# State-space layers: the LayerNorm's scale and shift on ScalarE between the next group's taps, with the shift made on GpSimd

## The reference

```python
def ssm_layer(x, Wi, cw, cb, Wo, g, b):          # x: (16, 128, 256), fp32
    proj = x @ Wi                                # 256 -> 512 + 64 + 64
    xs, Bm, Cm = proj[..., :512], proj[..., 512:576], proj[..., 576:]
    xc = silu(conv1d(xs, cw, 4 taps, causal) + cb)
    # h = -0.5 * h + u_t b_t ; y_t = h c_t, over the 128 steps
    return layer_norm(y @ Wo + x, g, b)
def layer_norm(x, g, b, eps=1e-05):
    mu = jnp.mean(x, axis=-1, keepdims=True)
    var = jnp.mean((x - mu) ** 2, axis=-1, keepdims=True)
    return (x - mu) * jax.lax.rsqrt(var + eps) * g + b
```

## Time and profile before

| | us |
|---|---|
| runs | 1495.00, 1495.44, 1496.55 (median 1495.44) |
| the profiled execution: its own time | 1493.37 |
| its span | 1491.6 |
| busy in the span: PE / DVE / ACT / POOL | 1207.3 / 841.1 / 631.7 / 603.6 |

### The profile page before, as it was taken

One profiled execution on the slowest core, in us unless ns is written; L12 is line 12 of the kernel. 1 busy time (PEld: TensorE's weight loads), 2 busy tenths in 40 slices (PEclk: granted clock), 3 DMA queues, 4 the chain that ended last, 5 costly groups with the idle time before them and its releaser, 6 DMA issues. The chain is left out here.

```text
span 1491.6 us, 21444 instructions
## 1 busy us (share of the span) xinstructions
PE 1207.3 (81%) x7243; PEld 944.3 (63%) x7243; DVE 841.1 (56%) x1844; ACT 631.7 (42%) x1863; POOL 603.6 (40%) x612
## 2 busy tenths in 40 slices
PE   4999999999799999997367777747999995366632
PEld 3888888888577777776356666544666663355521
DVE  6888888888434545444364754543222221448885
ACT  2555555555254454454136556612222221246420
POOL 2276767665521433333444534412111112644531
PEclk9999999999899999999688987867999998679865
DMA  4001010110000000000150002031111113210000
GB/s 143 1 15 54 15 53 15 52 27 3 0 1 1 1 1 1 1 2 1 34 227 2 1 2 85 1 142 32 47 46 44 49 43 83 90 43 15 15 14 29
DMA packets 30492, 53.38 MB, mean 36 GB/s; under 512 B 5088, under 2 KB 23264, under 8 KB 28864
## 3 DMA queue, kind: packets, MB, share of 16 engines
q1 hardware_dynamic: 26704, 39.72, 7.9%
q0 software_dynamic: 3408, 9.31, 2.2%
q10 hardware_dynamic: 288, 3.15, 0.6%
HBM read 42.86 MB, written 9.31 MB: 35 GB/s over the span
## 5 line engine op out<-in xcount | busy, mean ns | idle before, releaser
L414 DVE SCALAR_TENSOR_TENSOR ssm_conv<-bank,conv_w,ssm_conv 128x508 f32<-128x508 f32 (+2 forms) x240 | 159.2, 727 | 9.6 <-ACT ssm_conv L350 9.6
L1468 PE MATMUL bank<-expert_raw,e_rows_t 128*128 x312 | 148.9, 601 | 1.2 <-ACT e_rows_t L1540 1.2
L303 PE MATMUL bank<-w_out,ssm_u 128*128 128x256 f32 x640 | 143.5, 382 | 0.0
L710 ACT ACTIVATE a_prob<-bank,a_neg_max 128x128 f32<-128x128 f32 x256 | 90.5, 367 | 100.8 <-DVE a_neg_max L751 100.8
L303 PEld LDWEIGHTS bank<-w_out,ssm_u 128*128 128x128 f32 x640 | 119.9, 190 | 17.9
L1180 ACT ACTIVATE expert_raw<-bank,x_neg_max 128x128 f32<-128x128 f32 x256 | 90.9, 377 | 80.9 <-DVE x_neg_max L1114 80.9
L808 POOL TENSOR_TENSOR a_prob<-a_prob,a_inv 128x512 f32<-128x512 f32 x64 | 66.1, 1040 | 131.3 <-DVE a_inv L756 131.3
L1038 POOL TENSOR_TENSOR expert_raw<-expert_raw,x_inv 128x512 f32<-128x512 f32 x64 | 66.8, 1043 | 113.2 <-DVE x_inv L1120 113.2
L1415 POOL DMA_INDIRECT e_rows<-z_rows,e_index x39 | 37.1, 951 | 177.4 <-PE bank L1463 170.5
L1665 DVE COPY e_h_t<-bank 128x512 f32<-128x512 f32 x39 | 27.0, 692 | 128.0 <-PE bank L1477 128.0
L508 POOL TENSOR_TENSOR act_t_lo<-ssm_turned,act_t_hi 128x512 fp32r<-128x512 f32 x40 | 51.5, 1289 | 97.8 <-ACT ssm_turned L375 97.8
(11 more groups left out here) (360 smaller groups left out, 3209.7 us busy)
## 6 DMA issues: line engine op xcount, KB each, us to landing
expert_raw<-in_experts_laid SPq DMA_DIRECT2D x6, 1536.0 KB, 10.8
y_rows<-e_y SPq DMA_DIRECT2D x39, 128.0 KB, 1.7
attn_raw<-in_attn_w_laid SPq DMA_DIRECT2D x4, 1024.0 KB, 7.5
w_in_raw<-in_L_attn_in_proj_w SPq DMA_DIRECT2D x5, 640.0 KB, 8.4
expert_raw<-in_experts_laid ACTq DMA_DIRECT2D x2, 1536.0 KB, 8.7
w_out<-in_L_attn_out_proj_w SPq DMA_DIRECT2D x5, 512.0 KB, 3.4
x_res<-in_x SPq DMA_DIRECT2D x4, 512.0 KB, 5.6
expert_raw<-in_ctx_t_laid SPq DMA_DIRECT2D x4, 512.0 KB, 6.7
```

The lines of the kernel that those rows point to most:

```text
L303: mm = pe.matmul(UWY[h][:, s * D:(s + 1) * D], u[:, g % 2, c, t:t + P], w_out[:, c, :], start=(c == 0), stop=(c == KI - 1))
L414: op = dve.scalar_tensor_tensor(out=acc, in0=xs, scalar=conv_w[:, c, TAPS - 1 - back:TAPS - back], in1=acc, op0=ALU.mult, op1=ALU.add)
L710: e = act.activation(prob[:, m % 4, i, :], S[m % 2][:, i * P:(i + 1) * P], ACT.Exp, bias=neg_max[:, m % 4, i:i + 1], accum_out=total[:, m ...
L1468: mm = pe.matmul(bank[:, :], rows_t[:, t % 2, k, :], W[:, bass.ds(at + (column + k * FFN), FFN)], start=(k == 0), stop=(k == KD - 1))
```

## The change

DVE's four L450 instructions go. POOL makes minus the mean (a multiplication by a tile of -1), and after the `pow` the shift, minus the mean times rstd. ACT forms rstd * x + shift as four `ACT.Identity` instructions of 128x256 with scale and bias pointers, in the place `front` of the next group gives them: one behind tap 1, one behind tap 2, two behind tap 3. Where there is no next group they stand together: ahead of the last group's `copy_uw`, and at the very end. POOL, which waited for DVE's results by `z_ready`, now waits for ACT's by the same semaphore.

```diff
--- before.py
+++ after.py
@@ -179,6 +179,7 @@
     uw = sb("ssm_uw", [P, 2, 2 * D])
     res = sb("ssm_res", [P, 2, 2, D])
     stats, mv, ve = mem["stats"], mem["mv"], mem["ve"]
+    neg_mean, shift, neg_one = (sb("ssm_" + name, [P, GS]) for name in ("neg_mean", "shift", "neg_one"))
 
     bc_ready = sem("bc_ready")
     xs_ready = sem("xs_ready")
@@ -199,6 +200,7 @@
     aggr_ready = sem("aggr_ready")
     var_ready = sem("var_ready")
     rstd_ready = sem("rstd_ready")
+    neg_one_ready, neg_mean_ready, shift_ready = sem("neg_one_ready"), sem("neg_mean_ready"), sem("shift_ready")
     z_ready = sem("z_ready")
     zg_ready = sem("zg_ready")
     act_ready = sem("act_ready")
@@ -333,7 +335,13 @@
 
         @block.scalar
         def _(act):
-            def front(layer, g, first=False):
+            def normalise(layer, g, i):
+                n = layer * GROUPS + g
+                act.wait_ge(shift_ready, n * 2 + i // 2 + 1)
+                act.activation(res[:, i // 2, i % 2, :], res[:, i // 2, i % 2, :], ACT.Identity, bias=shift[:, i:i + 1],
+                               scale=ve[:, i:i + 1]).then_inc(z_ready, 1)
+
+            def front(layer, g, first=False, before=None):
 
                 n = layer * GROUPS + g
                 act.wait_ge(bc_ready, n + 1)
@@ -349,6 +357,9 @@
                         act.wait_ge(u_ready, n * KI - KI + c + 1)
                     nc.scalar.activation(conv[:, c, :], XS(c)[:, :], ACT.Identity, bias=conv_b[:, c:c + 1],
                                          scale=conv_w[:, c, TAPS - 1:TAPS]).then_inc(tap_last, 1)
+                    if before and c > 0:
+                        for i in ((0,), (1,), (2, 3))[c - 1]:
+                            normalise(*before, i)
 
             def silu(layer, g, chunks, first=False):
                 n = layer * GROUPS + g
@@ -381,13 +392,15 @@
                 first, last = layer_is(layer, 0), layer_is(layer, LAST)
                 for g in range(GROUPS):
                     ahead = (layer, g + 1, first) if g < GROUPS - 1 else None if last else (layer + 1, 0)
+                    before = (layer, g - 1) if g > 0 else None if first else (layer - 1, GROUPS - 1)
                     if ahead:
-                        front(*ahead)
-                    if ahead:
+                        front(*ahead, before=before)
                         silu(*ahead[:2], range(0, 2), *ahead[2:])
+                    else:
+                        for i in range(GS):
+                            normalise(*before, i)
                     copy_uw(layer, g, 0)
                     copy_uw(layer, g, 1)
-                    before = (layer, g - 1) if g > 0 else None if first else (layer - 1, GROUPS - 1)
                     if before:
                         copy_turned(*before, 0)
                     if ahead:
@@ -395,6 +408,8 @@
                     if before:
                         copy_turned(*before, 1)
             layers(act, layer_steps)
+            for i in range(GS):
+                normalise(LAST, GROUPS - 1, i)
             for h in range(2):
                 copy_turned(LAST, GROUPS - 1, h)
 
@@ -443,12 +458,6 @@
                     dve.wait_ge(aggr_ready, n * 4 + 2 * h + 2)
                     dve.tensor_scalar(ve[:, 2 * h:2 * h + 2], mv[:, 2 * h:2 * h + 2, 1], EPS, None,
                                       ALU.add).then_inc(var_ready, 1)
-                for h in range(2):
-                    dve.wait_ge(rstd_ready, n * 2 + h + 1)
-                    for s in range(2):
-                        i = 2 * h + s
-                        dve.tensor_scalar(res[:, h, s, :], res[:, h, s, :], mv[:, i, 0:1],
-                                          ve[:, i:i + 1], ALU.subtract, ALU.mult).then_inc(z_ready, 1)
 
             convolve(0, 0, 0)
             convolve(0, 0, 1)
@@ -471,9 +480,13 @@
 
                 n = layer * GROUPS + g
                 for h in range(2):
+                    pair = slice(2 * h, 2 * h + 2)
                     pool.wait_ge(var_ready, n * 2 + h + 1)
-                    pool.tensor_tensor(ve[:, 2 * h:2 * h + 2], ve[:, 2 * h:2 * h + 2], neghalf[:, 0:2],
-                                       ALU.pow).then_inc(rstd_ready, 1)
+                    pool.tensor_tensor(neg_mean[:, pair], mv[:, pair, 0], neg_one[:, pair], ALU.mult).then_inc(neg_mean_ready, 1)
+                    pool.tensor_tensor(ve[:, pair], ve[:, pair], neghalf[:, 0:2], ALU.pow).then_inc(rstd_ready, 1)
+                    pool.wait_ge(neg_mean_ready, n * 2 + h + 1)
+                    pool.wait_ge(rstd_ready, n * 2 + h + 1)
+                    pool.tensor_tensor(shift[:, pair], neg_mean[:, pair], ve[:, pair], ALU.mult).then_inc(shift_ready, 1)
                 if g == 0:
                     pool.wait_ge(names["ln_loaded"], layer * 32 + 32)
                 for h in range(2):
@@ -507,6 +520,8 @@
                     pool.wait_ge(tr_copied, n * 2 + h + 1)
                     pool.tensor_tensor(lo, turned[:, :, :], hi.bitcast(F32), ALU.subtract).then_inc(tr_low, 1)
 
+            pool.memset(neg_one[:, :], -1.0).then_inc(neg_one_ready, 1)
+            pool.wait_ge(neg_one_ready, 1)
             with pool.Fori(0, LAST) as layer:
                 for g in range(GROUPS):
                     finish(layer, g)
```

## The result

| | before | changed |
|---|---|---|
| median of 11 runs each, us | 1497.97 | 1501.88 |
| lowest and highest | 1495.00, 1499.49 | 1496.93, 1504.38 |
| ratio of the times | | 1.0027, 95% interval 1.0015 to 1.0039 |
| span of the profiled execution | 1491.6 | 1495.2 |

The change makes the kernel slower by 0.27%, between 2.2 and 5.8 us. The forecast was 1500.5 us on the three runs of before that were known then, 5.1 us of loss. The sign, the place and the size of that loss are in the trace.

The account below looks back on a forecast made before the run. PE was taken to bound the kernel. The profiled 1493.37 us plus 4.4 for stalls and 0.7 for the stage's end gave 1498.5, and the runs' median distance of 2.07 made it 1500.5 us; range 1497.5 to 1503.5.

Parts of the forecast that it names:

- DVE's part: In the groups, removing DVE's 80 instructions, median 892 ns, is worth 0 us, since they are hidden under PE's `project`.
- the rival that the 0.35 us ahead of L291 are a hidden wait for DVE: Ahead of the mixing products, freed DVE ends a 0.35 us wait 19 times, up to 6.6 us gained; chance 0.03.
- The shift: On POOL, four new small instructions make each half's shift ready 1.2 us apart, costing nothing in 19 groups.
- ACT's order: Between ACT's taps, the second instruction waits for tap 2, so POOL's first product starts 2.91 us later; taps don't slip.
- The stall: At `project` in layers 0 to 3, PE waits for late `w_in_lo`, 1.1 us each, 4.4 us in all.
- The end: At the stage's end, the open chain through POOL and ACT grows from 6.99 to 7.6 to 7.7 us, 0.7 more.
- The clock: At PE's stalls in layers 0 to 3, the granted clock stays 1.00, since stalls of 1.1 us are short.
- the rival: At the four stalls PE's clock falls, 2.3 us lost each, 9.2 us on top, 1509.7 us; chance 0.05.
- The whole: Whole kernel: 4.4 us of stalls plus 0.7 at the end, giving 1500.5 us; chance 0.80.

Follow-up runs that it names:

- e6: Kernel before with DVE's scale and shift left out and nothing in its place; middle 334.0 us, as before, and 346.0 with the end; one run.
- e7: Changed kernel with the shift made by DVE in one instruction per half instead of on POOL; 1.0044 of the kernel before, middle 338.6 us.
- e1: Changed kernel with ACT's four instructions earlier, two behind tap 0 and two behind tap 2; 1.0007 of the kernel before, middle 334.1 us.
- e4: Changed kernel with all four ACT instructions behind tap 3; 1.0128 of the kernel before, middle 350.4 us.
- e3: Kernel before with two extra POOL additions ahead of the input weight split in layers 0 to 3; 1.0012 of the kernel before, middle 336.9 us.
- e2: Changed kernel with POOL's input weight split ahead of the attention weight split; 1.0003 of the kernel before, middle 334.1 us.
- e8: e5 with half 1's last scale and shift on ACT and its shift made by DVE; 0.9990 of the kernel before.
- e5: Kernel before with the last group's end shared out: DVE finishes half 1, POOL half 0, DVE makes the last remainders; 0.9988 of the kernel before.

## Why the prediction was right

**DVE's part.** Worth nothing in the middle, as forecast; e6 takes it away and the middle stays at 334.0 us. This also settles the rival that the 0.35 us ahead of L291 are a hidden wait for DVE.

**The shift.** Forecast ready 1.2 us after POOL starts and of no consequence: it was, and e7 shows the no consequence. `pow` takes 0.71 us here, not 0.76, with the small instructions between.

**ACT's order.** Forecast: POOL's first product 1.36 us behind tap 2's start. Measured 1.35. e1 and e4 move just this place, and the loss goes away or grows. No tap slips in the changed kernel, and in e1, where tap 1 does, the middle stays at 334.1 us.

**The stall.** Forecast 1.10 us a layer, 4.4 in all; measured 1.21 to 1.22 in layers 1 to 3 and 0.94 in layer 0, 4.6 in all. Two small errors met: `w_in_lo` is 0.99 us behind where PE wants it in layer 2 (forecast 1.04), and the handover from POOL to PE takes 0.23 us in layers 1 to 3, not the 0.06 that I took from the earlier trace rows. In layer 0 `w_in_lo` ends at 90.31 and PE starts at 90.36, 0.05 us later. The same two values, to 0.02 us, come back in e3, e4 and e7. The three long ones are where PE waits in its hardware loop, whose awaited value comes from the loop's counter; no row shows whether that is the reason.

**The end.** Forecast 0.7, measured 0.6: from POOL's first small instruction to its first product 2.40 us, as forecast, and 7.57 us in all against 7.6 to 7.7.

**The clock.** Forecast to stay up, as a stall of 1.1 us is short: it is 1.00 from 57 us to 384 us in the changed kernel. e4 shows that the rival was real, only further off: the clock falls behind the stalls of 2.95 to 2.97 us, and not behind the one of 2.78. Whether the length or the moment decides, these four can't tell apart. The rival's price was too high as well: 1.56 us a stall, not the 2.3 taken from the stage's end. The Trainium skill (TensorE: Matmul & The Clock Gate, What's actually happening) has the clock fall only after a window of idle time, and has the window run free of the kernel. For the changed kernel the trace agrees. But by the Trainium skill a stall as short as e4's should leave the clock alone too; three did not, and the measurement decides.

**The whole.** The stage is 5.2 us longer in the trace. The medians differ by 3.9 us and the interval reaches from 2.2 to 5.8, which holds it. The profiled pair differs by 3.6 us in span: self-attention's first product comes at 401.02 instead of 395.74, 5.28 us later, and 1.7 us are given back behind it, in code that the change doesn't touch. Some 0.8 of it is the clock's. It is low when self-attention starts, and rises 4.8 us behind that start in the profile of before and 3.1 us behind it in the changed kernel's. Windows from 3 to 5 us behind the start, before and changed (granted clock in the third column from the end):

```profile
398.74:400.74 2.00, 2.00 (x6) 1.52 (x6) 0.00 (x0) 0.54 (x1) 0.00 (x0) 0.54 0.00 0
```

```profile
404.02:406.02 2.00, 2.00 (x9) 1.55 (x9) 0.49 (x1) 0.54 (x1) 0.00 (x0) 0.96 0.00 0
```

From self-attention's first product to its first with the causal mask it is 26.28 us before and 25.52 now; over the ten profiles it is 25.45 to 26.81. Neither this nor the other 0.9 us is shown to be the change's: see the last section.

The whole time came nearer than its parts. The forecast of 1500.5 us is 1.4 under the measured 1501.88, but it stood on the first three runs of the kernel before: with eight more their median rose by 2.5 us, to 1497.97, while the difference of the medians is 3.9 and not 5.1. That these two met is luck; the forecast of the stage, 5.1 against 5.2, is not.

## What to carry to other kernels

Work taken off an engine that the bound engine never waits for is worth nothing, however busy that engine is; but the work's results have readers, and its new place decides when they start. Ask what else stands in the reader's queue, and how much slack the last thing in it has: here 1.6 us of slack under a 2.6 us delay. Where such a queue holds both an urgent and a patient job, the order of the two is the cheapest repair (e2), though here it only brings the changed kernel back to the old one and not ahead of it. And in an in-order program an instruction "between" two others waits for whatever the later one of them waits for.

## What the runs showed of the hardware

- The stage repeats to 0.1 us between executions and chips (middle 334.0, 334.1, 334.1, 334.0, 334.0, 334.0, in the six kernels where PE never waits for `w_in_lo`), while the rest of the kernel, from self-attention's first product to the end of the span, took from 1094.2 to 1103.5 us in the ten profiles, with the same code. A few tenths of a per cent are better read from a distance inside the stage than from whole times.
- PE stalls of 0.6 to 1.2 us left the granted clock at 1.00 in all twelve cases (e3, the changed kernel, e7). In e4 stalls of 2.95 to 2.97 us brought it to 0.50 for some 3.5 us three times, one of 2.78 us did not: a stall's price jumped from its own length to its length and 1.6 us more.
- A DVE instruction that read two SBUF tensors was held up beside POOL as L450 was: 1.78 us against 0.69 for 128x512 (e8 and e5, one case each). POOL's own instructions took 1.26 to 1.30 us in both cases, so there it was DVE that waited. ACT's scale-and-shift took 0.59 us, alone or beside POOL: minimum 0.583, maximum 0.602 over 80 of them in the changed kernel.
- From POOL's end to the start of a waiting PE it took 0.04 to 0.05 us in the code of layer 0, which is written out, and 0.23 to 0.25 us in the hardware loop of layers 1 to 3, in four kernels alike (the changed one, e3, e4, e7).
- A POOL addition of 128x512 that reads one 128x128 tile four times over for both inputs took about 1.09 us, where those with two different full tiles took 1.27 to 1.30.
